# Message passing with layer norm over 100,000 nodes: x[src] gathered by tiles of the edge list instead of by blocks of nodes

## The chip, the cores and the metric

The kernel runs on one core of a Trainium2 chip. The metric is the device time of the whole program in microseconds (us), as the median of several runs; lower is better. Five engines work side by side, each through its own instructions in order: TensorE (PE), VectorE (DVE), ScalarE (ACT), GpSimd (POOL) and SyncE (SP, which here only issues DMAs). They wait for each other on semaphores.

## The reference

```
x: (100000, 48) f32   src, dst: (25000,) int32, sorted by dst   edge_attr: (25000, 32) f32
tmp = concat([x[dst], x[src], edge_attr], axis=1)        # 25000 x 128
h   = relu(tmp @ W1 + b1)                                # 128 x 128
msg = h @ W2 + b2                                        # 128 x 48
out = layernorm(x + segment_sum(msg, dst, 100000))       # no weight, no bias; eps 1e-5
```

The edges stand in the order of `dst`. `dst` and `src` are drawn at random, so about one node in four has an edge, and 128 edges reach over some 512 nodes.

## The kernel before

The 100,000 nodes are cut into 261 blocks of 384 nodes (the last has 160). Three blocks make a group; there are 88 groups, and one group is one step of every engine's loop. A block takes the 128 edges from its first edge on; edges that belong to a later block match no node of this one and count for nothing. Where a block has more than 128 edges, or `dst` isn't sorted, a flag (`general`) makes all engines run a slow general path at the end.

**Set-up.** `dst`, `src` and the edge attributes are loaded with 196 edges in a row on each partition. ACT copies the attributes and DVE and POOL the two indices into `table_pm`, whole rows of 34 numbers (32 attributes, dst, src), and SP stores them in four large DMAs as `edge_table` in DRAM (line 674). Meanwhile PE and DVE count, for each block, how many edges lie below it: that is the block's first edge (`first_edge`).

**A step.** Function `walk` gives each engine its stages with a lag in steps. `PEELED` = 2 rounds of 8 steps are written out, 64 steps run in a loop of 8 rounds, the rest is written out again. In step t:

- SP reads three first edges from SBUF into registers (line 681) and loads, for group t+3, three tiles of 128 table rows into `cat` (line 691); it loads the group's nodes `xs` for group t+2 (line 696, after the sums of group t-6 have left that buffer free); it stores the finished nodes of group t-9 (line 700, after POOL's scaling).
- POOL gathers x[src] for group t+2 with three indirect DMAs straight into `cat` (line 732); the row numbers are the last column of the rows that SP has just loaded, so the gather waits for them (`row_in`). Then it scales group t-8 by 1/std in one instruction (line 740).
- DVE makes a one-hot matrix of each block (1064), splits x into three bf16 parts (1070, 1075), splits the messages (1040, 1047), and does the sums of the layer norm (1024, 1033, 1082, 1090).
- PE turns `cat` of group t-2 (773) after `xsrc_in`, turns the one-hots (779), adds the messages of group t-5 to its nodes (819, 27 matmuls), multiplies by W1 (827), fetches x[dst] for group t-1 by one-hot matmuls (839, 27 matmuls), and multiplies by W2 (858) while it puts the nodes themselves in the sum (805).
- ACT carries the results from PSUM to SBUF.

Most buffers have 8 places (`BODY`), so an engine can be several steps away from another before it must wait.

Of the kernel before, what the change touches and what calls it, by code (L numbers as in the profile page):

```python
# [5 lines left out]
P = 128  # L6
F32 = mybir.dt.float32
# [7 lines left out]
META = 2  # L15
# [4 lines left out]
BLOCK = BP * J  # L20
# [6 lines left out]
PARTS = 3  # L27
assert PARTS == SUPER
# [346 lines left out]
def gnn_resnorm_kernel(nc, x, src, dst, edge_attr, W1, b1, W2, b2, out):  # L375
# [38 lines left out]
    PAD_PART = EREST // TC  # L414
    ROWS = P * EC
    LAST = ROWS - P
# [7 lines left out]
    edge_table = nc.dram_tensor("edge_table", (ROWS, DE + META), F32, kind="Internal").ap()  # L424
# [3 lines left out]
    with ExitStack() as ctx:  # L428
# [19 lines left out]
        src_pm = sb("src_pm", [P, EC], I32)  # L448
        edge_pm = sb("edge_pm", [P, EC, DE])
        table_pm = sb("table_pm", [P, EC, DE + META])  # L450
# [37 lines left out]
        cat = sb("cat", [P, BODY, SUPER, P + META])  # L488
# [31 lines left out]
        cols_placed = sem("cols_placed")  # L520
        attr_placed = sem("attr_placed")
        table_out = sem("table_out")
# [11 lines left out]
        xsrc_in = [sem(f"xsrc_in{s}") for s in range(BODY)]  # L534
        x_in = [sem(f"x_in{s}") for s in range(BODY)]
        y_out = [sem(f"y_out{s}") for s in range(BODY)]
        may_gather = sem("may_gather")
# [24 lines left out]

        def load_attributes(eng, c):

            attr_v = edge_attr[0:EP * EC, :].rearrange("(p t) d -> p t d", p=EP)
            for p0, p1 in ((0, EK), (EK, EP)):
                eng.dma_start(edge_pm[p0:p1, c * TC:(c + 1) * TC, :], attr_v[p0:p1, c * TC:(c + 1) * TC, :]).then_inc(attr_in[c], 16)

# [69 lines left out]
        def by_node(tile, g, s):  # L638
# [7 lines left out]
            xsq_in=[t[:, :, :].rearrange("p t c -> p (t c)") for t in (edge_pm, table_pm)],  # L646
# [4 lines left out]
        def _(sp):  # L651

            tables = (dst, dst_pm, dst_in), (src, src_pm, src_in)
            for table, idx, done in tables:
                full = table[0:EP * EC].rearrange("(p t) -> p t", p=EP)
                sp.dma_start(idx[0:PAD_P, :], full[0:PAD_P, :]).then_inc(done, 16)
                sp.wait_ge(pad_set, 3)
                sp.dma_start(idx[PAD_P:EP, :], full[PAD_P:EP, :]).then_inc(done, 16)
                sp.dma_start(idx[EP:P, 0:EREST], table[EP * EC:E].rearrange("(a t) -> a t", a=1)).then_inc(done, 16)
                if table is dst:  # L660
                    sp.dma_start(next_dst_i[0:EP, :], dst[EC:E].rearrange("(p t) -> p t", t=1)[0:(EP - 1) * EC + 1:EC, :],
                                 allow_slow_non_contiguous=True).then_inc(next_in, 16)
# [458 lines left out]
```

## Time and profile before

| | |
|---|---|
| median of 3 runs | 494.03 us (492.64 to 494.47) |
| span of the profiled execution | 593.7 us |
| instructions in the span | 19546 |
| busy: PE, DVE, POOL, ACT | 73%, 65%, 59%, 49% |
| chain that ended last: PE, "issue" | 66%, 18% |
| mean share of DMA engines in the steps | 43% |
| gathers (POOL) | 264, 1015 ns each |
| scalings (POOL) | 88, 912 ns each |

The profiled execution took 99.7 us longer than the median run. A stretch that the profile shows is therefore not simply a stretch of a run that is only timed, and the first thing to find out is which rows hold in both. Rows of SP in the timeline are its DMA issues; its register work stands between them and isn't counted as busy.

### The profile page before, as it was taken

The numbers are of one execution on the slowest core, as the hardware profiler recorded it, in microseconds if no ns is written. First come the engines' busy times: TensorE is split into PE (matmuls) and PEld (weight loads), VectorE is DVE, ScalarE is ACT, GpSimd is POOL, SyncE is SP. The second block draws the span as 40 slices with busy tenths as digits, with TensorE's granted clock in tenths as the row PEclk, the third lists the DMA queues.
The fourth block names the chain that finished last, engine by engine and source line by source line (L and its number), as shares of the span: only waits on it lengthen the run. The fifth ranks groups of instructions, "written<-read, shape, count | busy, mean of one in ns | idle before, by whom it ended". The sixth has DMA issues, their size and how long they took to land.

```text
span 593.7 us, 19546 instructions
## 1 busy us (share of the span) xinstructions
PE 430.8 (73%) x6796; PEld 368.5 (62%) x6796; DVE 383.0 (65%) x1105; ACT 292.1 (49%) x795; POOL 351.2 (59%) x365
## 2 busy tenths in 40 slices
PE   1013378797888878788788878787888878887891
PEld 1012367676767767676667767675776767766690
DVE  5423148676766678676667666776667756877673
ACT  2212147464555556464555545464555545554662
POOL 2056616767665666666665666666666666757522
PEclk9999999988988899898989888989889989999996
DMA  7833313444433434344444344343443434444422
GB/s 181 286 64 67 68 25 82 86 110 87 110 84 81 108 84 108 83 108 82 100 89 94 94 83 108 81 109 82 88 100 83 108 83 107 86 108 85 105 64 73
DMA packets 118243, 56.92 MB, mean 96 GB/s; under 512 B 46019, under 2 KB 117185, under 8 KB 118205
## 3 DMA queue, kind: packets, MB, share of 16 engines
q1 hardware_dynamic: 109440, 48.35, 32.2%
q0 software_dynamic: 8448, 6.50, 8.6%
q10 hardware_dynamic: 318, 1.61, 1.0%
q8 instruction: 20, 0.33, 0.2%
q14 instruction: 17, 0.14, 0.1%
HBM read 33.80 MB, written 22.61 MB: 95 GB/s over the span
## 4 chain that ended last, share of the span: by engine, by line
PE 66%; issue 18%; another core or an unknown queue 6%; ACT 4%; DVE 3%; DMA 1%; ACTq 0%; POOL 0%; SPq 0%; POOLq 0%; DVEq 0%
PE bank L839 14%; PE bank L827 11%; PE bank L819 10%; PE bank L779 8%; PE bank L805 8%; PE bank L858 7%; PE bank L773 7%; ACT onehot_t L899 2%; DMA next_dst_i<-in_dst_dram 1%; PE bank L851 1%; ACT sq L926 1%; ACT hid_t L915 1%; ACT cat L921 0%; ACT msg L894 0%
## 5 line engine op out<-in xcount | busy, mean ns | idle before, releaser
L732 POOL DMA_INDIRECT cat<-in_x_dram,cat x264 | 267.9, 1015 | 201.1 <-DMA cat<-edge_table 135.7
L899 ACT ACTIVATE onehot_t<-bank 128x384 bf16<-128x384 bf16 (+1 forms) x261 | 119.3, 498 | 182.1 <-remote 129.4
L1024 DVE TENSOR_REDUCE total<-bank 128x9 f32<-128x432 f32 (+1 forms) x88 | 52.8, 599 | 87.6 <-remote 86.5
L839 PE MATMUL bank<-x_low,onehot_t 128*128 128x48 bf16 (+1 forms) x782 | 86.0, 185 | 27.4 <-issue 26.9
L839 PE MATMUL bank<-x_rest,onehot_t 128*128 128x48 bf16 (+1 forms) x782 | 85.8, 186 | 26.7 <-issue 26.6
L858 PEld LDWEIGHTS bank<-w,hid_t 128*128 128x128 f32 x522 | 101.5, 208 | 4.0 <-issue 2.8
L779 PEld LDWEIGHTS bank<-ident_b,onehot 128*128 128x128 bf16 (+1 forms) x782 | 65.2, 107 | 61.4 <-issue 48.1
L839 PE MATMUL bank<-xs,onehot_t 128*128 128x48 bf16 (+1 forms) x782 | 86.6, 186 | 22.5 <-issue 22.1
L779 PE MATMUL bank<-ident_b,onehot 128*128 128x128 bf16 (+1 forms) x782 | 80.6, 236 | 24.9 <-issue 24.9
L740 POOL TENSOR_TENSOR ys<-ys,rstd 128x432 f32<-128x432 f32 (+1 forms) x88 | 80.3, 912 | 23.6 <-DVE rstd L1090 20.5
L858 PE MATMUL bank<-w,hid_t 128*128 128x48 f32 x522 | 89.9, 255 | 2.5 <-issue 2.5
L839 PEld LDWEIGHTS bank<-x_low,onehot_t 128*128 128x128 bf16 (+1 forms) x782 | 65.4, 97 | 34.5 <-issue 33.9
L839 PEld LDWEIGHTS bank<-x_rest,onehot_t 128*128 128x128 bf16 (+1 forms) x782 | 65.8, 97 | 32.5 <-issue 31.9
L827 PE MATMUL bank<-cat_t,w 128*128 128x384 f32 (+1 forms) x176 | 83.6, 559 | 1.0 <-issue 0.7
L839 PEld LDWEIGHTS bank<-xs,onehot_t 128*128 128x128 bf16 (+1 forms) x782 | 67.2, 97 | 26.3 <-issue 25.7
L1040 DVE TENSOR_TENSOR msg_rest<-msg 128x144 f32<-128x144 f32 (+1 forms) x88 | 27.1, 308 | 75.4 <-issue 37.6
L887 ACT ACTIVATE cat_t<-bank 128x384 f32<-128x384 f32 (+1 forms) x88 | 42.9, 487 | 64.1 <-PE bank L773 54.8
L819 PE MATMUL bank<-msg,onehot 128*128 128x48 bf16 (+1 forms) x782 | 73.7, 188 | 0.5 <-issue 0.5
L1064 DVE TENSOR_SCALAR onehot<-node_of,dst_in_block 128x384 bf16<-128x384 f16 x260 | 73.8, 338 | 0.1
L819 PE MATMUL bank<-msg_rest,onehot 128*128 128x48 bf16 (+1 forms) x782 | 73.0, 187 | 0.4 <-issue 0.4
L819 PE MATMUL bank<-msg_low,onehot 128*128 128x48 bf16 (+1 forms) x782 | 72.9, 187 | 0.0
L773 PE MATMUL bank<-ident,cat 128*128 128x128 f32 x261 | 52.6, 316 | 25.9 <-ACT cat L921 18.9
(91 smaller groups left out, 910.8 us busy)
## 6 DMA issues: line engine op xcount, KB each, us to landing
xs<-in_x_dram SPq DMA_DIRECT2D x86, 216.0 KB
out_dram<-ys SPq DMA_DIRECT2D x86, 216.0 KB
cat<-edge_table SPq DMA_DIRECT2D x264, 17.0 KB
cat<-in_x_dram,cat POOLq DMA_INDIRECT x264
edge_table<-table_pm SPq DMA_DIRECT2D x4, 833.0 KB, 7.5
edge_pm<-in_edge_attr_dram ACTq DMA_DIRECT2D x2, 686.0 KB, 6.0
edge_pm<-in_edge_attr_dram SPq DMA_DIRECT2D x2, 686.0 KB, 6.0
edge_pm<-in_edge_attr_dram ACTq DMA_DIRECT2D x2, 91.9 KB, 7.3
```

What stands on the lines that cost most here:

```text
L732: pool.indirect_dma_start(cat[:, v, k, D:2 * D], None, x[:, :], bass.IndirectOffsetOnAxis(ap=cat[:, v, k, P + 1:P + 2].bitcast(I32), axis= ...
L740: pool.tensor_tensor(y, y, rstd[0:n, v % SMALL, 0:blocks * jj].unsqueeze(2).broadcast_to([n, blocks * jj, D]), ALU.mult).then_inc(normed, 1)
L773: last = pe.transpose(cat_ps[:, k * P:(k + 1) * P], cat[:, v, k, 0:P], ident[:, :])
L779: last = pe.transpose(onehot_ps[k % 2][0:n, j * P:(j + 1) * P], onehot[:, v, k, j * n:(j + 1) * n], ident_b[:, :])
L805: pe.matmul(sum_ps[v % SMALL][0:n, 0:blocks * jj * D], ident_b[0:n, 0:n], part, start=(i == 0), stop=False)
L819: last = pe.matmul(ps[0:n, (k * jj + j) * D:(k * jj + j + 1) * D], onehot[:, v, k, j * n:(j + 1) * n], part[:, k * D:(k + 1) * D], start=F ...
L827: pe.matmul(hid_ps[:, 0:blocks * P], w1[:, :], cat_t[:, v % SMALL, 0:blocks * P], start=True, stop=True).then_inc(hid_done, 1)
L839: last = pe.matmul(xdst_ps[:, k * D:(k + 1) * D], onehot_t[0:n, v % SMALL, k, j * P:(j + 1) * P], part[:, (k * jj + j) * D:(k * jj + j + 1 ...
L858: last = pe.matmul(msg_ps[:, k * D:(k + 1) * D], hid_t[:, v % SMALL, k * P:(k + 1) * P], w2[:, :], start=False, stop=(k == blocks - 1))
L899: act.activation(onehot_t[0:n, v % SMALL, k, 0:jj * P], onehot_ps[k % 2][0:n, 0:jj * P], ACT.Copy).then_inc(onehot_t_ready, 1)
L1024: dve.tensor_reduce(total[0:n, v % SMALL, 0:blocks * jj], sums_of(g, v % SMALL), AX_X, ALU.add).then_inc(totalled, 1)
L1064: last = dve.tensor_scalar(onehot[:, v, k, 0:n * jj], nodes[:, 0:n * jj], dst_in_block[:, v % SMALL, k:k + 1], None, ALU.is_equal)
```

## The change

The table in DRAM gets rows of 81 numbers: x[src] (48), the attributes (32) and dst. They are built in SBUF in `rows`, edge by edge in order, 128 edges to a tile, 196 tiles:

- `src` and `dst` are loaded with one tile of 128 edges in a row, converted by DVE, turned by PE, and copied back by DVE: `src_cols` (row numbers for the gathers) and a column of `rows`.
- The attributes are loaded straight into `rows`, an edge of 128 bytes at a time, by ACT's queue; ACT's copies fall away.
- POOL gathers x[src] for a tile with one indirect DMA into `rows`: 196 in all. 42 stand ahead of the first scaling; later, up to three go with one group, each followed by the scaling of one block, since the scaling is now three instructions per group. After group 69 no gather is left. POOL's program has no loop now.
- SP stores the tiles three at a time (66 DMAs of 124 KB) in the place of the four large DMAs, three before the first load of rows and the others in the steps, one step ahead of the load that may need them. In each set of 8 steps there are 6 stores. Before each load of rows it waits for the stores that this group may reach.
- The three loads of rows per group bring 81 numbers in the place of 34, x[src] among them, so POOL's gathers into `cat` are gone, and PE waits for `row_in`.
- A group's first edges are clamped to what has been stored by then; where the clamp bites, the flag for the general path is set.

```
+GROUP = 3
+GROUPS_FIRST = 3
+LEAD = 15
+STORE_AHEAD = 1
...
+    NGROUPS = -(-EC // GROUP)
+    BODY_GROUPS = BODY * BLOCK * SUPER * E // (N * P * GROUP)
+    def groups_for(v):
+        return GROUPS_FIRST + v * BODY_GROUPS // BODY
...
+            sp.wait_ge(pad_set, 1)
+            for i, table in enumerate((src, dst)):
+                by_tile = table[0:WHOLE * P].rearrange("(t p) -> t p", p=P)
+                sp.dma_start(ends_tm[:, i, 0, :], by_tile[0:P, :]).then_inc(src_in, 16)
...
-            sp.wait_ge(cols_placed, 2)
-            for c in range(TCH):
-                sp.wait_ge(attr_placed, c + 1)
-                sp.dma_start(edge_table.rearrange("(p t) c -> p t c", p=P)[:, c * TC:(c + 1) * TC, :].rearrange("p t c -> p (t c)"),
-                             table_pm[:, c * TC:(c + 1) * TC, :].rearrange("p t c -> p (t c)")).then_inc(table_out, 16)
-            sp.wait_ge(first_done, 1)
-            sp.wait_ge(table_out, 16 * TCH)
+            def store_rows(g, r, v):
+                for q in range(groups_for(v - 1) if after(g, 1) else 0, groups_for(v)):
...
+                    sp.wait_ge(xsrc_in[s], 16 * GROUP * (r + q // BODY_GROUPS) + 16 * size)
+                    tiles = bass.ds(first * GROUP, size)
+                    sp.dma_start(table_v[:, tiles, :], rows[:, tiles, :]).then_inc(row_out[s], 16)
+            def wait_rows(g, r, v):
...
+                    sp.wait_ge(row_out[q % BODY_GROUPS], 16 * (r + q // BODY_GROUPS + 1))
...
-                    sp.dma_start(cat[:, v, k, 2 * D:P + META], edge_table[bass.ds(first, P), :]).then_inc(row_in[v], 16)
+                    sp.dma_start(cat[:, v, k, D:P + META], edge_table[bass.ds(first, P), :]).then_inc(row_in[v], 16)
...
-            walk(sp, ((-AHEAD, load_edges), (-X_AHEAD, load_nodes), (9, store)))
+            walk(sp, ((-AHEAD - STORE_AHEAD, store_rows), (-AHEAD, load_edges), (-X_AHEAD, load_nodes), (9, store)))
...
-            walk(pool, ((1 - AHEAD, gather_xsrc), (8, scale)))
+            pool.wait_ge(src_placed, 1)
+            gathered = 0
+            for g in range(NS):
+                until = min(EC, GROUP * groups_for(g + LEAD))
+                for t in range(gathered, until if g == 0 else gathered):
+                    gather_xsrc(t)
+                    gathered += 1
+                for k in range(shape_of(g)[1]):
+                    if gathered < until:
+                        gather_xsrc(gathered)
+                        gathered += 1
+                    scale_block(g, k)
...
-                pe.wait_ge(xsrc_in[v], 16 * SUPER * (r + 1))
+                pe.wait_ge(row_in[v], 16 * SUPER * (r + 1))
...
-                act.activation(table_pm[:, c * TC:(c + 1) * TC, 0:DE], edge_pm[:, c * TC:(c + 1) * TC, :],
-                               ACT.Copy).then_inc(attr_placed, 1)
+                tiles = slice(c * TC, min((c + 1) * TC, WHOLE))
+                act.dma_start(rows[:, tiles, D:D + DE], attr_v[:, tiles, :]).then_inc(attr_in[c], 16)
```

How it changes the order is seen best on SP. In the loop, a step of SP before, from the store of one group to the load of nodes in the next step (`ISA` is register work; `cat` is the tile of rows, `xs` and `ys` are nodes in and out):

```order
L700 DMA out_dram<-ys 128x3x144
L686 REGISTER_ALU
L681 ISA [waits cat_turned]
L681 TENSOR_LOAD first_edge
L681 ISA x6
L691 ISA
L691 DMA cat<-edge_table 128x34
L691 ISA
L691 DMA cat<-edge_table 128x34
L691 ISA
L691 DMA cat<-edge_table 128x34
L696 ISA [waits sum_done]
```

The same place in the changed kernel, in one of the 6 steps out of 8 that have a store of rows:

```order
L743 DMA out_dram<-ys 128x3x144
L710 ISA [waits xsrc_in3]
L710 REGISTER_ALU
L710 DMA edge_table<-rows 128x3x81
L728 REGISTER_ALU
L721 ISA [waits cat_turned]
L721 TENSOR_LOAD first_edge
L721 ISA x6
L734 ISA
L734 DMA cat<-edge_table 128x81
L734 ISA
L734 DMA cat<-edge_table 128x81
```

Between the store of nodes and the reading of the first edges stands one more DMA, with register work and a wait of its own; everything behind it is as it was.

On POOL, before, a step where the loop hasn't begun yet (`cat` is the target of the gather, `row_in3` says that SP's load of this group has landed):

```order
L732 DMA cat<-in_x_dram,cat 128x48 [waits row_in3]
L732 DMA cat<-in_x_dram,cat 128x48 x2
L740 TENSOR_TENSOR ys<-ys,rstd 128x432 [waits rstd_ready]
L732 DMA cat<-in_x_dram,cat 128x48 [waits row_in4]
```

And after, from the end of the 42 leading gathers to the second group's scaling (`rows` is the table in SBUF, `src_cols` holds its row numbers):

```order
L775 DMA rows<-in_x_dram,src_cols 128x48 [waits xsrc_in1]
L775 DMA rows<-in_x_dram,src_cols 128x48 x2
L785 TENSOR_TENSOR ys<-ys,rstd 128x144 [waits rstd_ready]
L785 TENSOR_TENSOR ys<-ys,rstd 128x144 x2
L775 DMA rows<-in_x_dram,src_cols 128x48 [waits xsrc_in2]
L785 TENSOR_TENSOR ys<-ys,rstd 128x144 [waits rstd_ready]
L775 DMA rows<-in_x_dram,src_cols 128x48
L785 TENSOR_TENSOR ys<-ys,rstd 128x144
L775 DMA rows<-in_x_dram,src_cols 128x48
L785 TENSOR_TENSOR ys<-ys,rstd 128x144
```

The gathers no longer wait for a load of SP, they stand singly between pieces of scaling, and only the gather six sets of three earlier can hold them up.

## Rows read from the trace of the kernel before

**Rows 1.** The page: the span, busy time by engine, the last chain by engine.
```profile
span 593.7 us, 19546 instructions
...
PE 430.8 (73%) x6796; PEld 368.5 (62%) x6796; DVE 383.0 (65%) x1105; ACT 292.1 (49%) x795; POOL 351.2 (59%) x365
...
PE 66%; issue 18%; another core or an unknown queue 6%; ACT 4%; DVE 3%; DMA 1%; ACTq 0%; POOL 0%; SPq 0%; POOLq 0%; DVEq 0%
```

**Rows 2.** Two windows: length; PE, PEld, DVE, ACT, POOL busy; PE clock; DMA share.
```profile
82.00:94.00 12.00, 11.90 (x226) 10.67 (x223) 8.32 (x25) 9.35 (x25) 2.56 (x3) 1.00 0.24 53
...
140.00:500.00 360.00, 292.59 (x4640) 251.21 (x4637) 250.05 (x715) 191.21 (x534) 234.74 (x236) 0.92 0.43 94
```

**Rows 3.** The chain in order of time: start, us, what; windows 0:100 and 560:594.
```profile
84.31 0.68 PE bank L819 x27
...
88.35 0.68 PE bank L819 x27
...
94.36 0.68 issue
...
562.46 0.68 PE bank L819 x27
...
566.49 0.68 PE bank L819 x27
```

**Rows 4.** Timeline of POOL: start, duration, instruction, idle time before it.
```profile
77.00 0.95 POOL L732 DMA_INDIRECT cat<-in_x_dram,cat  x1 [0.30 <-issue]
90.83 0.94 POOL L732 DMA_INDIRECT cat<-in_x_dram,cat  x1 [12.89 <-DMA cat<-edge_table]
92.08 0.95 POOL L732 DMA_INDIRECT cat<-in_x_dram,cat  x1 [0.30 <-issue]
...
305.72 0.92 POOL L740 TENSOR_TENSOR ys<-ys,rstd 128x432 f32<-128x432 f32 x1
...
558.48 0.95 POOL L732 DMA_INDIRECT cat<-in_x_dram,cat  x1 [0.30 <-issue]
```

**Rows 5.** Waits of PE, SP, POOL in 140:500: total us, times, longest.
```profile
PE bank L839 <- issue: 57.0, 121, 1.2
...
SPq L696 <- remote: 22.0, 30, 1.5
SPq L696 <- PE bank L819: 1.4, 1, 1.4
...
POOL cat L732 <- DMA cat<-edge_table: 77.4, 46, 3.1
```

**Rows 6.** Timeline of SP's DMA issues: start, duration, instruction.
```profile
85.02 0.39 SPq L696 DMA_DIRECT2D xs<-in_x_dram  x1
...
89.05 0.39 SPq L696 DMA_DIRECT2D xs<-in_x_dram  x1
...
441.02 0.38 SPq L696 DMA_DIRECT2D xs<-in_x_dram  x1
441.70 0.41 SPq L700 DMA_DIRECT2D out_dram<-ys  x1
444.27 1.40 SPq L691 DMA_DIRECT2D cat<-edge_table  x3
445.87 0.38 SPq L696 DMA_DIRECT2D xs<-in_x_dram  x1
```

**Rows 7.** Start and end: timeline rows, and SP's queue in the window 28:80.
```profile
18.77 0.30 DVE L993 CAST first_edge<-first_clamped 1x300 int32<-1x300 f32 x1
...
34.16 1.17 POOL L732 DMA_INDIRECT cat<-in_x_dram,cat  x1 [20.85 <-DMA cat<-edge_table]
...
584.80 0.67 POOL L740 TENSOR_TENSOR ys<-ys,rstd 128x288 f32<-128x288 f32 x1 [0.49 <-DVE rstd L1090]
585.81 0.34 POOL L740 TENSOR_TENSOR ys<-ys,rstd 80x96 f32<-80x96 f32 x1 [0.34 <-DVE rstd L1090]
...
q1 hardware_dynamic: 7520, 2.29, 21.4%
```

More of the change, by code:

```diff
@@ L413, in gnn_resnorm_kernel @@
     assert TC * TCH == EC
-    PAD_PART = EREST // TC
+    WHOLE = E // P
+    ETAIL = E - WHOLE * P
+    assert WHOLE == EC - 1 and 0 < ETAIL < P
     ROWS = P * EC
+    ROW = D + DE + META
     LAST = ROWS - P
@@ L447, in gnn_resnorm_kernel @@
         dst_pm = sb("dst_pm", [P, EC], I32)
[L448 to L450 removed]
+        ends_tm = sb("ends_tm", [P, 2, 2, P], I32)
+        ends_rows = sb("ends_rows", [P, 2, 2, P])
+        src_cols = sb("src_cols", [P, EC], I32)
+        rows = sb("rows", [P, EC, ROW])
+        reach_i = sb("reach_i", [1, NG * BG // SUPER], I32)
+        reach = sb("reach", [1, NG * BG // SUPER])
+        beyond = sb("beyond", [1, NS - 1])
+        beyond_most = sb("beyond_most", [1, 1])
         dst_rows = sb("dst_rows", [P, EC + 1])
@@ L645, in gnn_resnorm_kernel @@
             xa_in=[onehot[:, :, :, :].rearrange("p s b n -> p (s b n)").bitcast(F32), xs[:, :, :].rearrange("p s m -> p (s m)")],
-            xsq_in=[t[:, :, :].rearrange("p t c -> p (t c)") for t in (edge_pm, table_pm)],
+            xsq_in=[rows[:, t * (EC // 2):(t + 1) * (EC // 2), :].rearrange("p t c -> p (t c)") for t in range(2)],
             general=general, general_done=general_done))
@@ L751, in _ @@
             pe.wait_ge(consts, 5)
+            pe.wait_ge(ends_floated, 1)
+            for i in range(2):
+                pe.transpose(bank[5 + i][:, 0:P], ends_rows[:, i, 0, :], ident[:, :])
+                pe.transpose(bank[5 + i][:, P:EC], ends_rows[0:EC - P, i, 1, :], ident[0:EC - P, 0:EC - P]).then_inc(ends_turned, 1)
             pe.wait_ge(holder_ready, 1)
@@ L997, in _ @@
             note(dve.tensor_scalar(crowded[:, :], most[:, :], P + 0.5, None, ALU.is_gt))
+            note(dve.tensor_tensor(beyond[:, :], first_clamped[:, SUPER - 1:SUPER * (NS - 1):SUPER], reach[:, 0:NS - 1], ALU.subtract))
+            note(dve.tensor_reduce(beyond_most[:, :], beyond[:, :], AX_X, ALU.max))
+            note(dve.scalar_tensor_tensor(out=crowded[:, :], in0=beyond_most[:, :], scalar=0.5, in1=crowded[:, :],
+                                          op0=ALU.is_gt, op1=ALU.add))
             dve.wait_ge(fell_summed, 1)
```

128 lines of the change are left out of this document (79 added, 49 removed).

## The prediction

> **What bounds the kernel now.** I read the page first, then the chain in order of time, then the windows and the waits of each engine. The page says PE: 73% busy, 66% of the last chain, and 18% of that chain is "issue", time in which PE waited for nothing that is shown [rows 1]. 18% of 593.7 us is 107 us, and the profiled execution is 593.7 - 494.0 = 99.7 us longer than a timed run. These two numbers are close, so I ask where the issue time lies. The chain shows the 27 matmuls of the sums once per step. Early on two of them start 88.35 - 84.31 = 4.04 us apart, and near the end 566.49 - 562.46 = 4.03 us apart. In between, the 80 steps from 84.31 to 562.46 take 5.98 us each [rows 3]. What the two quick stretches have in common is POOL: its gathers pause from 77.95 to 90.83 us [rows 4], the first piece of issue time in PE follows at 94.36 [rows 3], and the last gather ends at 559.43 [rows 4]. In the long window between, PE stands still 57.0 us in the middle of the x[dst] matmuls, where it has nothing to wait for [rows 5]. So gathers and standstill go together in the profiled execution. I take the standstill to be for the most part a matter of being recorded, because without it the sum comes down to the timed median and with it it doesn't. If all 99.7 us lie in the 80 steps, a timed step takes (478.2 - 99.7) / 80 = 4.73 us; if the whole span is stretched evenly, 5.98 x 494.0 / 593.7 = 4.98 us.
>
> What takes 4.73 to 4.98 us in a timed step? Four candidates:
> - PE: 4.03 us at a granted clock of 1.00, and 4.03 / 0.92 = 4.38 us at the mean clock of the long window [rows 2, 3].
> - DVE: 250.05 us busy in 360 us, which is 360 / 5.98 = 60 steps: 4.2 us [rows 2].
> - POOL: gathers start 92.08 - 90.83 = 1.25 us apart, three of them and one scaling of 0.92 us make 4.67 us [rows 4].
> - SP: it is never "busy" on the page, but its step can be read from its issues. The quickest step of the loop runs from 441.02 to 445.87: 0.68 us to issue the load of nodes and get to the store, 2.57 us for the store, the reading of three first edges and their register work, 1.60 us for three loads of rows: 4.85 us [rows 6]. In the 360 us window SP waits 23.4 us in all, 0.4 us per step; the rest is its own work or standstill [rows 5].
>
> SP at 4.85 and POOL at 4.67 us are the two that fit the timed step. POOL waits 77.4 us for SP's loads in the window [rows 5], SP hardly for POOL. So I take SP's queue to be the bound of a timed run, POOL close behind it, and PE, the engine that the page names, third.
>
> **The change part by part.**
> *POOL.* 264 gathers become 196, so 68 x 1.25 = 85 us of its queue go. A scaling of 144 numbers is not in the trace; 96 numbers on 80 partitions take 0.34 us and 288 take 0.67 us [rows 7], so about 0.42 us, by the line between them. Three make 1.27 us in the place of 0.92. A step has 2.25 gathers on average: 2.25 x 1.25 + 1.27 = 4.08 us in the place of 4.67. That is below PE's 4.38, so POOL stops being a bound. What is late next is what decides: SP, not PE.
> *SP, the stores.* 66 stores of rows come in. Three replace the four large stores in set-up. By the order of the program 48 of the others fall in the 64 loop steps and 15 in the written-out steps. No such store with register addresses and a wait of its own is in the trace; the nearest is the load of nodes with what follows it up to the next issue, 0.68 us in the loop [rows 6], of the same three runs per partition. Where it is written out, an issue is 0.39 us [rows 6] and some 0.05 more. The low bound for a loop store is the bare issue, 0.38 us, the high bound 0.68 plus a wait for the store's landing. I take 0.65, since registers have to be worked out here as there. 48 x 0.65 + 15 x 0.44 = 31 + 7 = 38 us. It lies on SP's queue, which is the path. The bounds give 48 x 0.38 + 15 x 0.39 = 24 us and 48 x 0.9 + 15 x 0.5 = 51 us. Queued behind each store are the reading of first edges and the three loads of rows, which DVE and PE want.
> *SP, the waits.* The gathers run 15 groups ahead, so their wait is long fulfilled. The landing of a store is asked for one step after its issue, nearly 5 us later; I cost it at nothing, and what hides it is the step itself (load of nodes, store of nodes, next first edges). If that cover is gone, each costs up to 1 us in 3 steps of 4; that is in the high bound.
> *The loads of rows.* 128 runs of 324 bytes instead of 136. The count of runs is the same, and that sets SP's issue. For the DMA engines: packets of SP's queue took 0.214 x 52 x 16 / 7520 = 24 ns each early on [rows 7]. A step gets 288 more of them by the stores, 288 x 24 / 16 = 0.4 us, loses three quarters of a gather, and stands at 43% of 5.98 us [rows 2]. Hidden, with room.
> *PE.* `cat` is turned after one wait instead of two in a row: nothing to gain, since PE isn't the path.
> *Start.* Before, the first gather is at 34.16 [rows 7] and SP's first load 4 us ahead of it, once the four large stores have landed. Now gathers begin after the indices are turned, by my estimate at 11 us; nine take 9 x 1.25 = 11 us; landing, storing and landing again 5 to 7 us. That is 28 to 30 us for SP's first load, as before. The first edges are ready at 19 us before [rows 7]; six index loads and two conversions ahead of it make that 23, not late. The attributes are 25,000 packets of 128 bytes: 25,000 x 24 / 16 = 38 us of the DMA engines, but the first store needs only a quarter, and the seventh, near 50 us, needs them all. I cost the start at 0, with -3 and +10 as bounds. The 42 leading gathers end at 11 + 52 = 63 us; the first scaling is due at about 63 us in a timed run (nine steps after 30). At nothing too, with +4.
> *ACT* loses 6 us of copies that nothing waits for.
>
> A rule of the Trainium skill bears on the disputed term, whether SP's rows hold in a timed run. The trace has 0.38 to 0.41 us for one issue [rows 6]. The page "DMA: Bandwidth & Descriptors", section "Why a DMA increments its semaphore by 16 and not by 1", gives 512 sequencer cycles for one issued DMA on generations before the newest; at the 1.2 GHz of a sequencer this is an estimate of 0.43 us, so the cost would belong to the issue and not to the recording, and 63 stores would be at least 27 us. By the rows alone it is 24 to 51.
>
> **The sum.** 494.0 + 38 us. From this comes off what SP isn't the bound by: SP's 4.85 us is 0.12 above the 4.73 us of the first estimate, so its timed step is at most 4.73, and POOL's 4.67 could be what holds it; I take 0.1 us x 64 = 6 us off. 494.0 + 38 - 6 = 526 us, some 6.5% slower; with the bounds of the store 512 to 540.
>
> **The rivals.**
> 1. *SP isn't the bound; POOL was.* If recording adds to SP's register instructions, its timed step is shorter. For: there are some 25 short instructions in it, and a small fee on each would be enough. Against: POOL's rows alone add up to less than the timed median. The point from which it decides: SP's step plus 48 x 0.65 / 64 = 0.49 us must be under 4.73, so SP's timed step under 4.24 us, 13% less than its row. Then PE is next at 4.38, or DVE: 494.0 - 80 x (4.73 - 4.38) = 466 us. With PE's clock higher than 0.92 it may reach 455.
> 2. *SP lies between.* At 4.4 to 4.6 us the step grows to 4.9 to 5.1: 494.0 + 64 x 0.15 to 0.35 = 504 to 516 us. At 4.2 to 4.25 nothing changes, 491 to 496 us.
> 3. *The standstill by gathers is partly real.* If a third stays in timed runs (0.3 us per step of the 57.0 / 60 = 0.95), a quarter fewer gathers give back 0.1 us in 70 steps and 0.3 us in the last 18: 494.0 - 12 = 482 us, if SP allows it, else it takes 5 to 10 us off the 526. For: SP is slowed by it as well. Against: then the rows without it come out too long for 494.
> 4. *The change doesn't do what it says.* The clamp on first edges could bite and call the general path, which would add hundreds of us. The head start is three sets of 384 edges, and random edges stray by some 80 from the even line: 1 in 100.
>
> **How the numbers follow.** My forecast (SP is the bound, 512 to 540 us) gets 0.42, rival 2 above 500 us gets 0.12, its unchanged part 0.08, rivals 1 and 3 together 0.37, rival 4 0.01. What a measurement of this kernel can tell from no change is about 0.5%. So faster 0.37, same 0.08, slower 0.55. The likeliest case has 526 us, and 512 to 540 as its own range. Both signs hold much, so the range for 8 in 10 goes from 464 to 538: it leaves out the deepest of rival 1 and the top of the store's bounds.
>
> **What would show it.** Right: SP's rows have no waits left in the loop, the distance from its store of nodes to its loads of rows grows from 2.57 to about 3.2 us in three steps of four, PE and DVE wait for `cat` or `xs`, and POOL is idle between scalings. Wrong at the first step: PE's chain is unbroken while SP waits at the load of nodes for the sums. Wrong on standstill: issue time in PE remains as long with a quarter fewer gathers. The profiled span itself may even shrink, since it has fewer gathers to stand still for; only the timed median decides.

## The result, and the profile after

| | before | changed |
|---|---|---|
| median of the timed runs | 494.25 us | 539.41 us (538.9 to 541.0, 4 runs) |
| ratio, with its 95% interval | | 1.0939 (1.0904 to 1.0975) |
| span of the profiled execution | 593.7 us, 491.4 us in a second recording | 537.1 us |
| mean step of the 64 loop steps (SP's loads of nodes) | 5.013 us (second recording) | 5.525 us |

The changed kernel is 9.4% slower by the ratio. The sign is as forecast; the time is 13 us above the forecast and 1.4 us above the top of the range.

The page of the changed kernel, as [rows 1] for before: span, busy time, the last chain by engine and by line, and two groups.

```profile
span 537.1 us, 19761 instructions
...
PE 393.6 (73%) x6800; PEld 337.7 (63%) x6800; DVE 376.4 (70%) x1113; ACT 285.8 (53%) x791; POOL 312.6 (58%) x470
...
SPq 59%; issue 18%; PE 9%; DMA 6%; DVE 2%; POOL 2%; ACT 1%; POOLq 0%; DVEq 0%
SPq L721 21%; SPq L734 19%; SPq L739 6%; SPq L743 6%; SPq L710 5%; DMA xs<-in_x_dram 3%; PE bank L891 2%; PE bank L883 2%; POOL rows L775 1%; PE bank L869 1%; DMA ends_tm<-in_dst_dram 1%; PE bank L903 1%; PE bank L837 1%; PE bank L922 1%; DMA edge_table<-rows 1%
...
L785 POOL TENSOR_TENSOR ys<-ys,rstd 128x144 f32<-128x144 f32 (+1 forms) x261 | 116.8, 459 | 169.0 <-DVE rstd L1165 167.0
...
L1145 DVE TENSOR_TENSOR x_rest<-xs 128x432 f32<-128x432 f32 (+1 forms) x88 | 56.0, 636 | 121.7 <-DMA xs<-in_x_dram 121.6
```

SP's queue is 59% of the chain: reading first edges (L721), loads of rows (L734), loads and stores of nodes (L739, L743) and the new store (L710). VectorE waits 121.6 us for nodes that SP asks for late, and POOL stands idle 167 us between scalings. The same shows in the window 140 to 500, as [rows 2]: VectorE is busy 270.70 of 360 us, POOL 221.40.

```profile
140.00:500.00 360.00, 289.24 (x5083) 249.26 (x5082) 270.70 (x788) 210.19 (x590) 221.40 (x330) 0.98 0.57 129
```

SP's issues in the timeline, as [rows 6] (start, duration, instruction):

```profile
302.15 0.38 SPq L739 DMA_DIRECT2D xs<-in_x_dram  x1
302.81 0.41 SPq L743 DMA_DIRECT2D out_dram<-ys  x1
...
308.23 0.38 SPq L739 DMA_DIRECT2D xs<-in_x_dram  x1
308.92 0.41 SPq L743 DMA_DIRECT2D out_dram<-ys  x1
311.51 1.40 SPq L734 DMA_DIRECT2D cat<-edge_table  x3
313.11 0.38 SPq L739 DMA_DIRECT2D xs<-in_x_dram  x1
313.79 0.41 SPq L743 DMA_DIRECT2D out_dram<-ys  x1
314.59 0.40 SPq L710 DMA_DIRECT2D edge_table<-rows  x1
317.03 1.46 SPq L734 DMA_DIRECT2D cat<-edge_table  x3
318.79 0.38 SPq L739 DMA_DIRECT2D xs<-in_x_dram  x1
```

The step without a store of rows lasts 313.11 - 308.23 = 4.88 us, the next one, with a store, 318.79 - 313.11 = 5.68 us: 0.80 us for an issue that itself takes 0.40. Over the whole loop, 40 steps with a store last 5.66 us on average and 16 without one 4.95 us, 0.71 us less. The step that closes a round of the loop has a store as well and takes 6.1 us (302.15 to 308.23).

**The profile of before, recorded a second time.** The first recording had a span 99.7 us longer than a timed run, and much of the prediction went into that. I therefore had the same program recorded again (its expectation stands with the experiments). Page, windows 140 to 450 and 150 to 400, and two rows of the waits:

```profile
span 491.4 us, 19546 instructions
...
PE 386.5 (79%) x6796; PEld 325.1 (66%) x6796; DVE 443.9 (90%) x1105; ACT 290.6 (59%) x795; POOL 368.9 (75%) x365
...
DVE 47%; issue 19%; SPq 16%; DMA 5%; POOL 5%; PE 4%; DVEq 1%; ACT 1%; POOLq 0%
...
140.00:450.00 310.00, 268.62 (x4793) 225.60 (x4794) 307.58 (x735) 195.90 (x551) 259.37 (x247) 1.00 0.50 115
...
150.00:400.00 250.00, 216.53 (x3861) 181.53 (x3859) 250.00 (x596) 158.36 (x446) 209.51 (x199) 1.00 0.50 114
...
ACT std L931 <- DVE sq_total L1082: 131.2, 80, 1.9
...
SPq L700 <- POOL ys L740: 32.7, 25, 4.6
```

This is another picture than [rows 1, 2, 5]. VectorE is busy for the whole of the second window, 250.00 of 250.00 us, where [rows 2] has 250.05 of 360. PE's standstill in the x[dst] matmuls (57.0 us in [rows 5]) is gone; SP waits 32.7 us in 25 places for POOL's scaling, but only 1.0 us of that lies between 150 and 400 us: in the loop SP's queue has no pause either. Nor has POOL's: it is busy for 209.5 of these 250 us, 37.8 us are short gaps of 0.16 to 0.30 us around its gathers, and it waits 1.8 us. One recording had shown a program in a rhythm that its timed runs don't have.

### The profile page after: what moved, and what is told of

Read it like the earlier page. It is cut to its first block, busy times and chain, and to the rows that moved or that the text cites. A ratio compares the mean times of both kernels' runs of the same rounds, so it can differ in the third digit from the quotient of the medians.

```text
span 537.1 us, 19761 instructions
## 1 busy us (share of the span) xinstructions
PE 393.6 (73%) x6800; PEld 337.7 (63%) x6800; DVE 376.4 (70%) x1113; ACT 285.8 (53%) x791; POOL 312.6 (58%) x470
## 3 DMA queue, kind: packets, MB, share of 16 engines
q0 software_dynamic: 6272, 4.83, 8.3%
## 4 chain that ended last, share of the span: by engine, by line
SPq 59%; issue 18%; PE 9%; DMA 6%; DVE 2%; POOL 2%; ACT 1%; POOLq 0%; DVEq 0%
SPq L721 21%; SPq L734 19%; SPq L739 6%; SPq L743 6%; SPq L710 5%; DMA xs<-in_x_dram 3%; PE bank L891 2%; PE bank L883 2%; POOL rows L775 1%; PE bank L869 1%; DMA ends_tm<-in_dst_dram 1%; PE bank L903 1%; PE bank L837 1%; PE bank L922 1%; DMA edge_table<-rows 1%
## 5 line engine op out<-in xcount | busy, mean ns | idle before, releaser
L785 POOL TENSOR_TENSOR ys<-ys,rstd 128x144 f32<-128x144 f32 (+1 forms) x261 | 116.8, 459 | 169.0 <-DVE rstd L1165 167.0
L775 POOL DMA_INDIRECT rows<-in_x_dram,src_cols x196 | 193.5, 987 | 36.5 <-issue 26.1
L1145 DVE TENSOR_TENSOR x_rest<-xs 128x432 f32<-128x432 f32 (+1 forms) x88 | 56.0, 636 | 121.7 <-DMA xs<-in_x_dram 121.6
L987 ACT ACTIVATE sq<-ys 128x432 f32<-128x432 f32 (+1 forms) x88 | 49.3, 560 | 123.5 <-DVE ys L1108 123.2
L869 PE MATMUL bank<-xs,ident_b 128*128 128x432 bf16 (+1 forms) x88 | 31.7, 360 | 52.2 <-DVE ys L1108 50.3
L903 PE MATMUL bank<-xs,onehot_t 128*128 128x48 bf16 (+1 forms) x782 | 69.7, 185 | 0.0
L903 PE MATMUL bank<-x_rest,onehot_t 128*128 128x48 bf16 (+1 forms) x782 | 69.4, 184 | 0.0
L903 PE MATMUL bank<-x_low,onehot_t 128*128 128x48 bf16 (+1 forms) x782 | 69.3, 184 | 0.0
L883 PEld LDWEIGHTS bank<-msg,onehot 128*128 128x128 bf16 (+1 forms) x782 | 64.7, 97 | 0.1
L883 PEld LDWEIGHTS bank<-msg_rest,onehot 128*128 128x128 bf16 (+1 forms) x782 | 63.2, 98 | 0.1
```

The lines of the kernel that those rows point to most:

```text
L775: pool.indirect_dma_start(rows[:, t, 0:D], None, x[:, :], bass.IndirectOffsetOnAxis(ap=src_cols[:, t:t + 1], axis=0)).then_inc(xsrc_in[s], 16)
L785: last = pool.tensor_tensor(y, y, rstd[0:n, v % SMALL, m].unsqueeze(2).broadcast_to([n, jj, D]), ALU.mult)
L883: last = pe.matmul(ps[0:n, (k * jj + j) * D:(k * jj + j + 1) * D], onehot[:, v, k, j * n:(j + 1) * n], part[:, k * D:(k + 1) * D], start=F ...
L903: last = pe.matmul(xdst_ps[:, k * D:(k + 1) * D], onehot_t[0:n, v % SMALL, k, j * P:(j + 1) * P], part[:, (k * jj + j) * D:(k * jj + j + 1 ...
L1145: dve.tensor_tensor(flat_of(x_rest, g, v), flat_of(xs, g, v), upper_half(flat_of(xs, g, v)), ALU.subtract).then_inc(x_rest_ready, 1)
```

## The experiments

Where an edit is shown, lines of SP's and ACT's programs are cut to what moves. "Loop step" is the mean of the 64 loop steps of the recorded execution, from SP's loads of nodes. e6, e7, e14, e15 and e16 leave out a part of the work, as said below; the others compute everything.

| run | median (range), us | ratio to before (95%) | loop step |
|---|---|---|---|
| e1: change, row stores on ACT | 506.36 (505.36 to 509.05) | 1.0267 (1.0226 to 1.0308) | 5.119 |
| e2: before, 66 idle stores on SP | 532.75 (530.17 to 534.13) | 1.0787 (1.0744 to 1.0831) | 5.447 |
| e3, e11: before, node stores on ACT | 493.54 and 493.97 (479.41 to 495.05) | | 4.844 |
| e4: change, row and node stores on ACT | 468.82 (466.95 to 471.28) | 0.9501 (0.9456 to 0.9546) | 4.671 |
| e6: before, one gather in three left out | 485.12 (483.6 to 486.0) | 0.984 (0.9807 to 0.9874) | 4.949 |
| e7: e6, node stores on ACT | 423.31 (417.54 to 424.1) | 0.8532 (0.8457 to 0.8607) | 4.100 |
| e8: e4, row stores two steps ahead | 458.71 (455.28 to 461.88) | 0.9328 (0.9274 to 0.9382) | 4.474 |
| e9: change, scaling in one piece | 536.37 (534.96 to 536.87) | 1.0843 (1.081 to 1.0877) | 5.492 |
| e10: e8, scaling in one piece | 458.02 (456.97 to 458.77) | 0.9264 (0.9235 to 0.9292) | 4.527 |
| e12: change, most attributes later | 539.56 (537.16 to 540.36) | 1.0952 (1.0902 to 1.1002) | 5.506 |
| e13: e3, scaling on VectorE | 439.81 (439.33 to 440.3) | 0.8901 (0.8885 to 0.8917) | 4.321 |
| e14: e3, no scaling | 411.81 (411.07 to 412.38) | 0.8328 (0.8309 to 0.8346) | 4.006 |
| e15: before, no scaling | 479.49 (478.22 to 481.68) | 0.9713 (0.9677 to 0.9749) | 4.948 |
| e16: e8, no scaling | 426.91 (420.85 to 429.24) | | 4.111 |

e3 and e11 are one program, and its ten executions have two levels, 479.4 to 480.2 (three, both recorded ones among them) and 493.3 to 495.1 (seven). The loop step of 4.844 us is one of the quicker level.

**SP's stores, taken off and put on.**

```
-    walk(sp, ((-AHEAD - STORE_AHEAD, store_rows), (-AHEAD, load_edges), ...
+    walk(sp, ((-AHEAD, load_edges), ...
+    walk(act, ((-AHEAD - STORE_AHEAD, store_rows), (7, root), ...
```

> The changed kernel with one edit: the 66 stores of table rows are issued from ScalarE's queue instead of SyncE's; same data, same DMAs, same order of landings to wait for. Theory (SyncE's issue time is the bound, and the stores are what was added to it): in the trace of the changed kernel a loop step of SyncE takes 5.66 us with a row store and 4.90 without, so 48 x 0.75 + 15 x 0.5 = 43 us go, 539 - 43 = 496 us, give or take 5, since ScalarE is busy issuing the attribute loads until 31 us and the first stores may come 3 us later. Rival (the traffic is the bound: 324-byte rows, 166,360 packets instead of 118,243, nodes landing late): nothing is taken from the traffic, so 530 to 540 us.

e1 takes 33 us off the changed kernel and leaves it 13 us slower than before, 10 us above what was expected. Its recorded spans say where that lies: 13.1 us up to the nodes of group 18 (the first load of rows is at 38.0 us, before at 29.5), 6.8 us in the loop, and 4.0 us come back at the end (the recorded execution is 3 us above the median). In the loop SP waits 0.3 us, so its queue still sets the step. By the traces its reading of the three first edges into registers takes 1.10 us a step there, 1.03 before and 0.93 in the changed kernel; why it differs stays open. e2 is the counterpart: before with the 66 stores, in the same places and sizes, from SBUF to a table that nobody reads. Its four large stores stay, no gather is saved.

```
+    sp.dma_start(table_v[:, bass.ds(first * GROUP, size), :], spare[:, 0:size, 0:81]).then_inc(spare_out[...], 16)
+    walk(sp, ((-AHEAD - 1, store_rows), (-AHEAD, load_edges), ...
```

> The kernel before with one addition: SyncE issues the changed kernel's 66 row stores at the same places in its order (6 in 8 steps, 3 tiles of 128 x 81 numbers each, a register address and a wait that is always fulfilled, landing asked for one step later), but from an idle piece of SBUF to a DRAM tensor that nobody reads. Gathers, scaling and tables are those of before. Theory (SyncE is the bound before as well): 494 + 43 + 2 = 539 us, 4 less for each 0.06 us of slack that SyncE's step has. If SyncE had slack to GpSimd's 4.67 us step: 520 to 530. Rival (the loss comes from the longer rows, the packed attribute loads and the start): 494 to 502.

It comes out at 533 us, 6 below the sum of its theory. The stores alone make 39 us of the 45 between the two kernels. Together with e1: it is the place in SP's queue that costs, not the traffic, which is the same on ACT's.

**Node stores off SP's queue.** Their 0.41 us and the wait for the scaling go to ACT (`store` moved from `walk(sp, ...)` to `walk(act, ...)`), in before (e3, e11) and in e1's kernel (e4).

> The kernel before with one edit: the 88 stores of finished nodes are issued from ScalarE's queue instead of SyncE's. SyncE's step falls from about 4.9 to 4.3 us. Theory (SyncE is the bound of the kernel before, GpSimd with 4.67 to 4.70 us right behind): only 0.1 to 0.2 us per step, 480 to 488 us. Rival (GpSimd was the bound before): 494, within 2 us. Rival (TensorE was it, at 4.38 us and above): 494 as well.

> The kernel before with its 88 node stores issued by ACT, once more, unchanged. Its four executions took 479.4 and three times 493 to 495 us. If the two values are two ways in which the same program runs (which VectorE instruction meets a gather), both turn up again in six executions. If 479 was an accident, all six lie at 492 to 496 us, as two co-bounds at one height would have it.

> The changed kernel with both edits: row stores and node stores are issued from ScalarE's queue. SyncE's step falls from 5.53 to 4.3 us, GpSimd's is 4.1, VectorE's busy time 4.2, TensorE's 4.03 at full clock. Theory: the gain that the gathers were to bring shows once SyncE is out of the way: 496 - 64 x (4.95 - 4.4) - 24 x 0.4 = 451, say 450 to 465 us. Rival (traffic): above 500. Rival (ScalarE becomes the bound with two more issues per step, 3.3 + 0.9 us and its waits): 465 to 490.

SP now has slack, as this row of its waits in e3 shows, recorded in an execution of the quicker level: 74.7 us for the sums, in 73 steps.

```profile
SPq L696 <- PE bank L815: 74.7, 73, 4.4
```

Yet the step falls only from 5.01 to 4.84 us, and the median stays at 493.5, where 480 to 488 were expected. So SP's queue isn't the only bound of before: another stands at nearly the same height. In the changed kernel, with neither kind of store on SP, 469 us come out, 4 us above the expected range. That value lies in the range of the rival that ScalarE is the bound, but ScalarE waits 50.4 us for VectorE's sums between 150 and 400 us, while VectorE is busy for 246.4 of the 250. The change does take something off that other bound.

**The gathers.** e6 and e7 leave out x[src] of the third block of each group (those columns of `cat` are zero), 88 gathers fewer; e5 is the recording that was shown above.

> The kernel before, unchanged, looked at once more. In its first profiled execution (span 593.7 us against 494 timed) all engines stood still for some 0.7 us at a time while gathers ran; in five profiles of other kernels, two of which have the same gathers, nobody stood still. Theory (the standstill is an accident of that one recording): a span near 492 us with no issue time inside TensorE's x[dst] matmuls. Rival (the standstill belongs to this kernel when it is recorded): 585 to 600 us again.

> The kernel before with the third gather of each group left out (x[src] of the third block is zero, so the output is wrong in those rows); everything on SyncE as before. GpSimd's step falls from 4.67 to 3.4 us, and VectorE has one gather less to be held up by. Theory A (SyncE's 4.9 us step bounds the kernel before too, level with what GpSimd's gathers cost): 485 to 494 us. Theory B (GpSimd or VectorE behind the gathers is the only bound): 455 to 470 us.

> As the run with the third gather left out (x[src] of the third block is zero), and in addition the node stores are issued from ScalarE's queue. Theory A (two bounds at the same height, SyncE's queue and the gathers): neither edit alone gains, both together do: 450 to 465 us, VectorE's 4.3 us or TensorE's 4.1 to 4.4 being next. Theory B: as without the second edit, since SyncE never was a bound. Rival C (TensorE bounds at 4.8 us in timed runs): 490 with each.

Either relief alone gives 0 to 8 us in the median (14 on the quicker level of e3), both together some 70 us: two bounds at nearly one height. e7's 423 us lies 27 below its expectation, which had VectorE next at 4.3 us. It looked as if the other bound were POOL's queue of gathers. The timeline of VectorE shows a second candidate. First before (second recording), VectorE and then POOL; the three one-hots of 0.31 us each take 1.97 us together and end 0.13 us after POOL's scaling:

```profile
300.70 0.30 DVE L1040 TENSOR_TENSOR msg_rest<-msg 128x144 f32<-128x144 f32 x1
300.91 1.97 DVE L1064 TENSOR_SCALAR onehot<-node_of,dst_in_block 128x384 bf16<-128x384 f16 x3
302.80 0.20 DVE L1090 RECIPROCAL rstd<-std 128x9 f32<-128x9 f32 x1
...
300.87 0.95 POOL L732 DMA_INDIRECT cat<-in_x_dram,cat  x1 [0.30 <-issue]
301.83 0.92 POOL L740 TENSOR_TENSOR ys<-ys,rstd 128x432 f32<-128x432 f32 x1
302.91 1.12 POOL L732 DMA_INDIRECT cat<-in_x_dram,cat  x1 [0.16 <-issue]
```

Then e3, where it is the instruction on 3 numbers that lasts 1.15 us, up to the end of the scaling (304.88 and 304.91):

```profile
301.75 0.77 DVE L1064 TENSOR_SCALAR onehot<-node_of,dst_in_block 128x384 bf16<-128x384 f16 x3
...
303.76 1.15 DVE L1054 TENSOR_TENSOR dst_in_block<-cat,block_start 128x3 f32<-128x3 f32 x1
304.83 0.60 DVE L1070 TENSOR_TENSOR x_rest<-xs 128x432 f32<-128x432 f32 x1
...
303.96 0.92 POOL L736 TENSOR_TENSOR ys<-ys,rstd 128x432 f32<-128x432 f32 x1
305.04 1.25 POOL L728 DMA_INDIRECT cat<-in_x_dram,cat  x1 [0.16 <-issue]
306.59 0.94 POOL L728 DMA_INDIRECT cat<-in_x_dram,cat  x1 [0.30 <-issue]
307.84 0.94 POOL L728 DMA_INDIRECT cat<-in_x_dram,cat  x1 [0.30 <-issue]
308.79 0.93 POOL L736 TENSOR_TENSOR ys<-ys,rstd 128x432 f32<-128x432 f32 x1
```

From 150 to 400 us I added up what VectorE's instructions last beyond the undisturbed duration of their kind. In before it is 59.9 us in 50 steps, 1.2 us a step, in 50 instructions, all one-hots that end within 0.15 us of a scaling's end. In e3 it is 51.4 us in 52 steps, again one instruction each step, again at the scaling's end. e6 has 1.13 us a step, e7 0.23, e4 0.71, e8 0.65, the changed kernel 0.24. VectorE's busy time per step without it is 5.01 - 1.20 = 3.81 us in before, 4.84 - 0.99 = 3.85 in e3 and 3.84 in e7. In e7 a scaling held VectorE in only some 18 of 62 steps.

These differences don't yet say that the hold-up is what sets the step. In e6 SP's queue sets it (4.949 us with 1.0 us of waits in the loop, as in e15 below), and there the hold-up is 1.13 us, just what VectorE's own 3.82 us leave of the step: a hold-up can fill slack that is there anyway. And in e3 two queues have no pause, VectorE's and POOL's. Window and waits of POOL, 150 to 400 us:

```profile
150.00:400.00 250.00, 226.24 (x4022) 193.80 (x4020) 250.00 (x622) 165.40 (x463) 209.28 (x207) 1.00 0.53 118
...
POOL cat L728 <- issue: 40.0, 156, 0.3
```

209.28 us of work and 40.0 us of short gaps are 249.3 of 250 us, and by the timeline above POOL needs 308.79 - 303.96 = 4.83 us a step without one wait. So the second bound of before is one of these two, or both through each other: VectorE with 3.85 us and about 1 us of hold-up, or POOL's queue. e7 relieves both.

**The hold-up tested.** In e14, e15 and e16 nobody divides by the standard deviation: the last factor of the layer norm is left out. In e13 VectorE does it, so that kernel computes everything. Shown are the lines that e13 and e14 move, against e3; the wait of VectorE for a finished scaling (`normed`) goes as well.

```
-    walk(pool, ((1 - AHEAD, gather_xsrc), (8, scale)))
+    walk(pool, ((1 - AHEAD, gather_xsrc),))
-    walk(dve, ((6, total_sum), ...
+    walk(dve, ((8, scale), (6, total_sum), ...
```

> Before with node stores issued by ACT (493.6 us, 479.4 in its quickest executions, 4.84 us per step there) and the scaling done by VectorE itself, so that GpSimd has nothing but its 264 gathers. If GpSimd's scaling holds VectorE for about 1 us per step, VectorE's step becomes 3.85 us of its own and 0.6 us for the scaling, 4.45: 479.4 - 80 x 0.39 = 448 us (440 to 456). If the gathers hold it, VectorE has 0.6 us more work and the same hold-up: 4.84 + 0.55 = 5.4 us per step, 520 to 530 us.

> As the one before, but with no scaling anywhere: the nodes are stored without the division by the standard deviation (the last step of the layer norm is left out), and 264 gathers stay. If the scaling holds VectorE, its step falls to about 3.85 us, and PE (4.03 us at full clock), SyncE (about 4.0) or GpSimd's gathers (3.75) set the step: 479.4 - 80 x 0.75 = 419 us (412 to 430). If the gathers hold it, VectorE's step stays at 4.84: 475 to 495 us. If GpSimd's queue of 4.67 us was the second bound, it falls to 3.75 and the time as well, but then the VectorE instruction that is 1 us too long stays in the trace.

> Before with no scaling anywhere (the division by the standard deviation is left out), node stores on SyncE as they were. VectorE's hold-up is gone if the scaling makes it, but SyncE's queue of about 4.85 us per step stays: 480 to 490 us. A result near 420 would say that SyncE's queue was no bound of the kernel before.

> The version with all rows' and nodes' stores on ACT and the row stores two steps ahead (458.7 us, 4.47 us per step), with no scaling anywhere (the division by the standard deviation is left out). Its VectorE instructions last 0.65 us per step longer than their like. If the pieces of scaling are the cause, the step falls to 3.85 to 4.05 us and the whole to 420 to 432 us. If it is the gathers, which in this kernel also meet VectorE, it stays at 450 to 459.

All four come out in the range of the theory that the scaling holds VectorE, or less than 1 us beside it. VectorE gets 88 instructions of 0.59 us more in e13, and the kernel becomes 11% faster than before. Its page and chain, then those of e14 and e15:

```profile
span 437.5 us, 19356 instructions
...
PE 374.2 (86%) x6796; PEld 328.4 (75%) x6796; DVE 399.2 (91%) x1193; ACT 291.2 (67%) x795; POOL 273.8 (63%) x277
...
DVE 63%; issue 18%; SPq 8%; DMA 4%; PE 3%; ACT 1%; DVEq 1%; ACTq 0%
```

```profile
span 410.3 us, 19260 instructions
...
PE 83%; SPq 5%; DMA 4%; ACT 2%; DVE 2%; issue 2%
```

```profile
SPq 47%; issue 16%; DMA 14%; PE 11%; DVE 6%; ACT 5%; DVEq 0%; ACTq 0%
...
DVE x_rest L1062 <- DMA xs<-in_x_dram: 90.1, 85, 4.5
...
302.80 1.40 SPq L691 DMA_DIRECT2D cat<-edge_table  x3
304.39 0.38 SPq L696 DMA_DIRECT2D xs<-in_x_dram  x1
305.04 0.41 SPq L700 DMA_DIRECT2D out_dram<-ys  x1
```

With 264 gathers still there, VectorE's excess falls from 0.99 us a step (e3) to 0.06 in e13 and 0.13 in e14, and PE is the bound of e14 at 4.0 us a step, as [rows 3] have it at full clock. So it is for the most part the scaling that holds VectorE, not the gathers. But e13 and e14 also take 0.92 us off POOL's queue, so they don't separate the two candidates of before. The kernel that does is e10 (described below): POOL has slack there, 41.3 us of waits for VectorE's `rstd`, SP and PE have some as well, and VectorE alone has no pause, 249.34 of 250 us, with 0.68 us a step of hold-up:

```profile
150.00:400.00 250.00, 234.71 (x4298) 205.30 (x4297) 249.34 (x663) 176.95 (x496) 176.01 (x175) 1.00 0.73 157
...
POOL ys L784 <- DVE rstd L1197: 41.3, 15, 3.7
```

e8, its sister, falls from 4.474 to 4.111 us a step when the scaling goes (e16). So in these kernels the hold-up does set the step. For before that is argued, not shown.

e15 isolates SP: with no hold-up and VectorE waiting for nodes, SP's own loop step is 4.948 us, hardly under the 5.013 of before. So before stands at SP's bound. The other one is 0.1 us below it in e3's quicker level (4.84 us); on the level of 494 us, which was never recorded, it must be about as high.

**The change with its brake off.** e8 is e4 with the stores of rows two steps ahead (`STORE_AHEAD = 2`), the first three from SP, and the last group of rows filled up to three tiles. e10 and e9 put the scaling back in one piece, behind the group's gathers.

> The changed kernel with row stores and node stores on ScalarE's queue (as in the run that took 469 us), the row stores issued two steps ahead of the load instead of one, and the first three from SyncE (ScalarE issues attribute loads until 31 us). SyncE waited 46 + 18 us there for stores to land, 21 of them at the start. Two gathers of padding more. Theory: most of the 43 us in the loop go, but VectorE's 4.3 us step is next: 455 to 463 us. Rival (VectorE and its waits were the bound there already): 466 to 470 us.

> The changed kernel with its other part undone: each group is scaled in one instruction again, behind the group's gathers. If SyncE's queue is the bound of the changed kernel, the scaling doesn't matter, since GpSimd stands idle for 169 us of the changed kernel's span: within 1% of it, 534 to 545 us, beside 494 for the kernel before. If the three pieces cost or gain something by the way they stand between VectorE's instructions, it shows as more than 1% either way, and as a changed mean duration of VectorE's one-hots (0.309 us in the changed kernel).

> The version with row stores two steps ahead on ACT and node stores on ACT (458.7 us), with the scaling in one instruction for each group. There SyncE has slack and VectorE makes half of the chain. If the small pieces keep GpSimd's work from running into VectorE's, one piece is slower: 465 to 475 us. If only the sum of GpSimd's work counts, one piece of 0.92 us in the place of three of 0.46 saves 0.4 us of a queue that has slack: within 1% of 458.7 us, or a little faster.

e8 beats before by 6.7%. The three pieces do nothing for it (458.7 and 458.0 us; the excess of VectorE is 0.65 and 0.68 us a step) and cost the changed kernel some 3 us (539.4 against 536.4). And where both bounds are away, the rebuilt table is a loss: e16 takes 426.9 us (420.9 to 429.2), e14, with its 264 gathers, 411.8. By their recordings 7.7 us of that lie ahead of the nodes of group 18 and 6.7 in the loop.

**The start.** e12 asks for three quarters of the attributes only once the third store of rows has landed.

```
     act.dma_start(rows[:, tiles, D:D + DE], attr_v[:, tiles, :]).then_inc(attr_in[c], 16)
+    if c == 0:
+        act.wait_ge(row_out[2], 16)
```

> The changed kernel with the last three quarters of the attributes asked for only after the third store of rows has landed. It looks at the start alone, where the changed kernel's first load of rows is at 35.8 us and that of the kernel before at 29.5. If the 25,000 short packets of the attributes hold up the first stores and SyncE's issues there, the first load comes at 28 to 31 us and the landing of the third store falls from 7 us to 2 to 3. The remaining attributes then arrive 30 us later, and the seventh store waits for them, so the whole may still take 535 to 545 us. If the chain of nine gathers and two landings is what takes the time, the first load stays at 34 to 36 us.

SP's first load of rows (L734), in the changed kernel and then in e12; and in the changed kernel, ahead of it, a load of weights on SP and the loads of attributes on ACT:

```profile
2.18 21.83 ACTq L941 DMA_DIRECT2D rows<-in_edge_attr_dram  x3
24.04 7.27 ACTq L942 DMA_DIRECT2D rows<-in_edge_attr_dram  x1
...
5.74 6.07 SPq L686 DMA_DIRECT2D w<-in_L_gnn_W_dram  x1
...
35.80 1.43 SPq L734 DMA_DIRECT2D cat<-edge_table  x3
```

```profile
29.73 1.44 SPq L734 DMA_DIRECT2D cat<-edge_table  x3
```

The 6.1 us come from the loads of the attributes. Putting these off brings nothing: ACT is issuing until 50 us there, and the load of nodes of group 18 is at 128.6 us, against 129.2 in the changed kernel. A load of weights takes 5.9 us to issue in e12 too, with a quarter of the attributes under way.

## Why the prediction was off, point by point

*The bound.* "I take SP's queue to be the bound of a timed run, POOL close behind it." SP is right for the changed kernel and, at 4.948 us, within 0.07 us for before. "POOL close behind it" isn't refuted: in e3 its queue runs without a wait at 4.84 us, since the first gather behind a scaling takes 1.25 us where 0.95 is usual, and whether it or VectorE's hold-up sets that step is open. What the prediction had too low is VectorE, at 4.2 us a step from [rows 2]. That row is from the disturbed recording; the second one has VectorE busy without a pause, at 5.01 us a step, 1.20 of them hold-up. The same error, with its sign turned, sits in "gathers and standstill go together". The quick stretches and the gathers' pause in [rows 3, 4] were one observation, the program behind them had a further repeating event (the scaling), and the second recording of the same kernel, with all its gathers, has no standstill. That it was for the most part no part of a timed run was right; that recording as such makes it was wrong.

*The sum.* From the second recording of before to that of the changed kernel the span grows by 45.7 us. Its pieces, beside the terms of the sum:

| | forecast | measured |
|---|---|---|
| first load of rows | 0 | 35.8 - 29.5 = +6.3 |
| from there to the nodes of group 18, steps written out | +7 (15 stores) | 93.4 - 82.4 = +11.0 |
| 64 loop steps: stores | 48 x 0.65 = +31 | (5.525 - 4.948) x 64 = +36.9 |
| 64 loop steps: what SP wasn't the bound by | -6 | -(5.013 - 4.948) x 64 = -4.2 |
| from the nodes of group 82 to the end | 0 | 54.3 - 58.6 = -4.3 |
| sum | +32 | +45.7 |

The path and the mechanism held: in the loop of the changed kernel SP never waits, and its step grew by its stores. The step that failed is the size of two terms. The first is "48 x 0.65": against the step of e15 a store with registers and a wait costs 0.77 us (36.9 / 48), within the changed kernel 0.71 between steps with and without one, and 0.80 in the two steps of the timeline. It has more register work around its 0.40 us issue than the load of nodes that I priced it by (0.68, [rows 6]). The second is "I cost the start at 0": +6.3 us, and +4 more in the written-out steps. Its bound of +10 was stated, but the top of the range, 538, took in hardly any of it beside the store's bound. By e12 start and written-out steps aren't two independent terms: shortening one lengthened the other.

*The waits.* At nothing, for a store that lands within a step: nearly right in the changed kernel, where SP's step is long. Where SP is quick it is not: in e4 SP waits 46.0 us for the landing of stores in 22 places, 21.1 of them at once at the start, and two steps ahead (e8) 14.7 us.

*Loads of rows of 324 bytes:* hidden, as forecast. Three of them take 1.40 to 1.46 us of SP against 1.40. *POOL:* 0.459 us for a piece of scaling against the 0.42 of the estimate; it is idle 169 us in the changed kernel, so neither counts there. *The Trainium skill's figure* for an issue (page "DMA: Bandwidth & Descriptors", section "Why a DMA increments its semaphore by 16 and not by 1") agrees with the bare issue, an estimate of 0.43 us beside 0.40 in the rows, and leaves out the register work around it, which nearly doubles the price.

*The rivals.* Rival 1 (SP not the bound, 466 us) fell: e2 costs 39 us. It had a true core that the prediction couldn't see: with the stores on ACT the changed kernel takes 469 us. Rival 3 fell with the second recording: its standstill is no part of a timed run. The chance for slower, 0.55, was low for a path that could be counted row by row; much of it was lost on explaining the recording.

## To carry to other kernels

Before pricing a change, find every engine whose own work plus its hold-ups fills the step: here SyncE's queue (4.95 us), GpSimd's (4.84) and VectorE (3.85 and 1.0 to 1.2 of hold-up) stood side by side, each relief alone gave 0 to 15 us, node stores and scaling together gave 82 (e14). A hold-up can fill slack, so its length isn't yet what it costs; take it away in a kernel where the other queues do wait. Count DMAs per queue as you count instructions per engine, at the price between one issue and the next, and give new ones to the queue with slack. Where a recording is a fifth longer than the timed runs, record again before reading its causes.

## What the hardware showed beyond that

GpSimd's multiplication in SBUF (0.92 us) holds some VectorE instructions until it ends and lets others run. In all traces but the first of before I took the VectorE instructions that began inside a scaling, at least 0.15 us from its ends. Longer than their like by over 0.08 us were 22 of 22 `msg_low`, 29 of 29 `msg_rest`, 14 of 17 `x_low` and 5 of 6 `x_rest`, all with both operands in SBUF. None was among 209 `total` and 172 `ys`, which read PSUM, 61 `sq_total` and 22 `rstd`, with one operand from SBUF. Of `dst_in_block`, with two operands of 3 numbers, it was 41 of 148. The Trainium skill says this on the page "SBUF — State Buffer", section "SBUF: two separate sides": GpSimd and VectorE share one pair of ports that is locked for a whole instruction, and VectorE wants it in its quick modes or with two inputs in SBUF. The traces agree for these kinds, with 22 of 22 and 0 of 172. By that page whoever starts first has the pair; in e3 `dst_in_block` is shown to start 0.20 us ahead of the scaling and is held all the same, and whether its shown start is its real one stays open.

Gathers hold the one-hots too, but briefly. In e14, where nobody scales, the 26 one-hots between 150 and 400 us that began 0.40 to 0.45 us ahead of a gather's end lasted until 0.08 us after it, 0.17 to 0.23 us longer than their like. In before, the held one-hot of each step begins 0.43 to 0.50 us ahead of a gather's end, and the scaling follows 0.02 us behind that gather. Of its 1.20 us of hold-up the scaling is 0.92; the rest belongs, by this likeness, to the gather ahead of it.

Open too is the pair of levels in e3. Both recorded executions were quick, with a hold-up of 0.99 us a step in `dst_in_block`; before has 1.20 in the one-hots, and 0.2 us in 80 steps, 16 us, is close to the 14 to 15 us between the levels. That is argued, not shown: no execution at 494 us was recorded.

The first recording of before was never seen again: none of the spans recorded since lies more than 2.2 us below its time.
